# Two of the five sums of convolution weights made by an adding transfer on GpSimd's queue, and a second-level difference moved up on VectorE

## The chip, the cores and the metric

The kernel runs on one core of one Trainium2 chip. Its engines are named as in the profile: PE (TensorE, matrix products), PEld (its weight loads), DVE (VectorE), ACT (ScalarE), POOL (GpSimd) and SP (SyncE, which issues transfers). The metric is the device time of one execution in microseconds; 289.74 us is the median of three runs before the change (289.65 to 289.8).

## The reference, cut to what matters

64 graphs of 128 nodes with 128 features go through a layer norm with ReLU, one graph layer and a residual sum. The part that the change touches is the second convolution of the layer, with 17 taps along the nodes:

```python
h = relu(bn1(conv1d(hT, conv1_w, pad=0)))          # 1 tap
h = bn2(conv1d(h, conv2_w, pad=8))                 # 17 taps, 128 -> 128 channels
x_conv = relu(h + hT)
s = x @ w_se.T + b_se ;  A = exp(-|s_n - s_m|^2) * adj
x_nmp = A @ relu(x @ w_msg.T + b_msg)
# GRU gates r, z, n from [x_conv, x_nmp] and x ; out = x + (1-z)*n + z*h
```

All is fp32. The kernel reaches that accuracy by splitting each factor of a product into a high part (float32r) and a low rest, and makes three products of each (high x high, high x low, low x high).

## The kernel before, in words

The graphs are worked on in 8 groups of 8. Each group's convolution is a two-level fast FIR scheme: instead of 16 taps on every node, sums and differences of weights and of inputs make nine smaller convolutions of four taps (`sub_conv(g, q)`, q from 0 to 8, L1277 to L1306), of which each is 12 or 15 matmuls with 256 columns; tap 16 rides along in some of them. The weights for them stand in `wt_hi` and `wt_lo` and are made once, in the set-up, while group 0 is already under way. They come in 13 lots (`LOTS`, L224 to L238): ACT writes the high part of lot n (`lot_high(n)`, L432 to L448) and DVE the low part (`lot_low(n)`, L786 to L790), which waits for the high part. Of the sources, lots 6, 7, 9 and 10 are raw weights of the tile `w2`; lots 2, 3 and 4 come from `fbb` and `fb`, pairwise sums (three DVE instructions, L1041, L1045, L1047); lots 5 and 8 come from `fab`, the sums of taps 4k+r and 4k+r+2 for r = 0 and r = 1, which DVE makes in two instructions of 128x512 (`sums_of_four(0)` and `sums_of_four(1)`, L1052 to L1063). The tiles `fb`, `fbb`, `fab` and `wg` lie in the tile `gate`, so the profile names them gate.

The input side of the scheme, for group 0: `cp` is the output of the first convolution with padding (ACT, L504); `level2_b` makes `vtb` (two DVE instructions, L842), `level1` makes `u` (L834, L835), `level2_u` makes `vtu` (L848, L849). ACT writes the high parts `v_hi` (`v_high_b`, L508; `v_high_u`, L520), DVE the low parts `v_lo` (`v_low_b`, L851; `v_low_u`, L861). `sub_conv(0, 3)` needs lot 5 and the first `v_low_u`; `sub_conv(0, 4)` the second, which follows ACT's `v_high_u(0, 1)` (L531).

Every engine's order is written out by hand and each engine runs in its order. ACT's around the change: lot 4, two copies `hg` (L474), lot 5, `v_high_u(0, 0)` (L526), `m_shared(0, 0)` (L541), lots 6 to 10, `v_high_u(0, 1)` (L531), messages. DVE's: L1047, lot 1, the first sum of four, lot 2, `v_low_b(0, 0)`, the two of `level2_b`, lot 3, `v_low_b(0, 1)`, lot 4, the second sum of four, `level1`, lot 5, `v_low_u(0, 0)`, `join_b`, lot 6, `level2_u`, `v_low_u(0, 1)`, `join_b`, lot 7, `v_low_u(0, 2)`, lot 8, the eleven small instructions of `distances` (L260 to L279), lot 9, and the joins of the output (L890 to L909). PE between: sub-convolutions 0 to 2, messages (L1236, L1240), 3 to 5, transposes of `slots` (L1251, which need `distances`), 6, distance products (L1264), 7 (which needs the first join L909), 8.

SP issues all big loads at the start, on one queue: two halves of `xin`, `w_a`, taps 0 to 7 of `w2`, taps 8 to 16, `wg` (w_gate), `bias`, `mask`; and once the first rows are normalised `xin` for group 1 and two tiles `xt`. POOL has nothing after the subtraction of `row` at L416 until the variances of group 1 (`ln_scale_first(2)`, L418).

Of the kernel before, what the change touches and what calls it, by code (L numbers as in the profile page):

```python
# [7 lines left out]
ALU = mybir.AluOpType  # L8
# [52 lines left out]
def gnn_kernel(nc, x_first, x_nm, x_t, adj_t, w_in, w_conv, w_gate, par_in, row_in, bias_in, ln_rows, out):  # L61
    ctx = ExitStack()
    with ctx:
        def sb(name, shape, dt=F32):
            return ctx.enter_context(nc.sbuf_tensor(name, shape, dt))

        def sem(name):
            return ctx.enter_context(nc.semaphore(name))
# [63 lines left out]
        w2 = sb("w2", [P, TAPS, P])  # L132
# [5 lines left out]
        fab = early[:, 21 * P:29 * P].rearrange("p (k r c) -> p k r c", r=2, c=P)  # L138
# [7 lines left out]
        xt_landed = [sem(f"xt_landed{i}") for i in range(3)]  # L146
        rows_stored, col_landed = sem("rows_stored"), sem("col_landed")
        out_stored = [sem(f"out_stored{c}") for c in range(NCH)]

        idle_set = sem("idle_set")  # L150
        pool_set, ident_ready, pool_par, par_ready, row_ready, pads_set = (
            sem("pool_set"), sem("ident_ready"), sem("pool_par"), sem("par_ready"), sem("row_ready"),
            sem("pads_set"))
        row_split, sums_ready, wt_hi_ready, wt_lo_ready = (
            sem("row_split"), sem("sums_ready"), sem("wt_hi_ready"), sem("wt_lo_ready"))
# [37 lines left out]
        def every(first, count, step=2):  # L193
            return slice(first, first + step * (count - 1) + 1, step)
# [4 lines left out]
        def cols(c):  # L199
            return slice(c * CW, (c + 1) * CW)  # L200
# [7 lines left out]
        def part_of(pair, p):  # L208
            return pair[0][:, :] if p == 0 else pair[1][:, (p - 1) * QW:p * QW]
# [7 lines left out]
        def stored(k, n=1):  # L217
            return wt_hi[:, k:k + n, :], wt_lo[:, k:k + n, :]

        raw16 = w2[:, 0:16, :].rearrange("p (k r) c -> p r k c", r=4)  # L220
        fbk = fb.rearrange("p (k r) c -> p r k c", r=2)
        fabk = fab.rearrange("p k r c -> p r k c")
# [60 lines left out]
        @block.sync  # L283
        def _(sp):
            sp.dma_start(xin[:, 0:4, :], x_first[0, :, 0:4, :]).then_inc(xh_landed, 16)
            sp.dma_start(xin[:, 4:8, :], x_first[0, :, 4:8, :]).then_inc(x_landed, 16)
            sp.dma_start(w_a[:], w_in).then_inc(wa_landed, 16)
            sp.dma_start(w2[:, 0:8, :], w_conv[:, 0:8, :]).then_inc(w2a_landed, 16)
            sp.dma_start(w2[:, 8:TAPS, :], w_conv[:, 8:TAPS, :]).then_inc(w2b_landed, 16)
            sp.dma_start(wg, w_gate).then_inc(wg_landed, 16)  # L290
            sp.dma_start(bias[:], bias_in).then_inc(bias_landed, 16)
            sp.dma_start(mask[:], adj_t[0]).then_inc(mask_landed, 16)

            def column_rows(g):

                sp.wait_ge(scale_ready, g - 1)

                upto(sp, col_landed, 16 * (g - 2))
                sp.dma_start(ln_rows.rearrange("k (p b) -> p k b", b=GB), scale[:]).then_inc(rows_stored, 16)
                sp.wait_ge(rows_stored, 16 * (g - 1))  # L300

                sp.wait_ge(wt_lo_ready, LOT_OF_GATES)
                if g > 2:
                    sp.wait_ge(hf_ready, NCH * g)
                sp.dma_start(col_ln, ln_rows.unsqueeze(0).broadcast_to([P, 2, GW])).then_inc(col_landed, 16)


            sp.wait_ge(hn_ready, NCH)
            sp.wait_ge(hn_first, 2)
            sp.dma_start(xin[:], x_first[1]).then_inc(x_landed, 16)  # L310
            for g in range(2):
                sp.dma_start(xts[g][:], x_t[g]).then_inc(xt_landed[g], 16)

            sp.wait_ge(a_ready, NCH)
            sp.dma_start(mask[:], adj_t[1]).then_inc(mask_landed, 16)

            sp.wait_ge(hn_ready, 2 * NCH)
            sp.wait_ge(hn_first, 3)
            sp.dma_start(xin[:], x_nm[0]).then_inc(x_landed, 16)

            sp.wait_ge(ht_ps, 2 * NCH)
            sp.dma_start(xts[2][:], x_t[2]).then_inc(xt_landed[2], 16)
            sp.wait_ge(stats_ready, 3)
            sp.dma_start(xin[:], x_nm[1]).then_inc(x_landed, 16)
            column_rows(2)
            for g in range(1, NG):
                sp.wait_ge(out_ready, NCH * (g - 1) + 1)
                sp.dma_start(out[g - 1, :, cols(0)], ob[0]).then_inc(out_stored[0], 16)
                if g + 2 < NG:

                    sp.wait_ge(sum_ready, NCH * g)
                    sp.dma_start(xts[(g + 2) % 3][:], x_t[g + 2]).then_inc(xt_landed[(g + 2) % 3], 16)
                sp.wait_ge(out_ready, NCH * (g - 1) + 2)
                sp.dma_start(out[g - 1, :, cols(1)], ob[1]).then_inc(out_stored[1], 16)
                if g + 1 < NG:
                    sp.wait_ge(a_ready, NCH * (g + 1))
                    sp.dma_start(mask[:], adj_t[g + 1]).then_inc(mask_landed, 16)
                if g + 3 < NG:
                    sp.wait_ge(stats_ready, g + 3)
                    sp.dma_start(xin[:], x_nm[g + 1]).then_inc(x_landed, 16)  # L340
                if g + 2 < NG:
                    column_rows(g + 2)
            for p in range(3):
                sp.wait_ge(out_ready, LAST + p)
                sp.dma_start(out[NG - 1, :, PART_COLS[p]], part_of(ob, p)).then_inc(out_stored[min(p, 1)], 16)
            sp.wait_ge(out_stored[0], 16 * NG)
            sp.wait_ge(out_stored[1], 16 * (NG + 1))

        @block.gpsimd
        def _(pool):  # L350
# [17 lines left out]
            def ln_scale_first(step):  # L368

                tiles = (slice(0, 4), slice(4, GB), slice(0, GB))[step]  # L370
                pool.wait_ge(vpe_first, step + 1)
                if step == 2:

                    pool.wait_ge(hn_ready, NCH)
                    pool.wait_ge(hn_first, 2)
                pool.tensor_tensor(rstd[:, tiles], vpe[:, tiles], neg_half[:, tiles], ALU.pow).then_inc(rstd_first, 1)  # L376
# [37 lines left out]
            pool.wait_ge(row_ready, 4)  # L414
            pool.wait_ge(pool_par, 8)
            pool.tensor_tensor(row[32:33, :], row_raw[32:33, :], row_hi[32:33, :], ALU.subtract).then_inc(row_split, 1)  # L416
            pool.wait_ge(row_split, 3)
            ln_scale_first(2)  # L418
            pool.wait_ge(rstd_first, 3)
# [7 lines left out]
        def _(act):  # L427
# [4 lines left out]
            def lot_high(n):  # L432
                source, first, count = LOTS[n]
                if n == 0:
                    act.wait_ge(wa_landed, 16)
                elif n == 1:
                    act.wait_ge(w2b_landed, 16)
                elif n == 2:
                    act.wait_ge(sums_ready, 3)
                elif n == 5:  # L440
                    act.wait_ge(sums_ready, 4)
                elif n == 6:
                    act.wait_ge(w2a_landed, 16)
                elif n == 8:
                    act.wait_ge(sums_ready, 5)
                elif n == 11:
                    act.wait_ge(wg_landed, 16)
                act.activation(wt_hi[:, first:first + count, :], source, ACT.Copy).then_inc(wt_hi_ready, 1)  # L448
# [194 lines left out]
            ln_rows_first(0)  # L643
            h_rows_first()
            lot_high(1)
            act.wait_ge(pool_par, 5)
            act.wait_ge(pads_set, 2)
# [97 lines left out]
        def _(dve):  # L745
# [92 lines left out]
            def level2_b(g, i):  # L838
                if i == 0:
                    dve.wait_ge(c_ready, NCH * g + NCH)  # L840
                    upto(dve, v_lob_ready, 2 * g)
                dve.tensor_tensor(vtb[:, i], cp[:, every(1 + 4 * i, VN, 4), :], cp[:, every(3, VN, 4), :],  # L842
                                  ALU.subtract).then_inc(vtb_ready, 1)
# [202 lines left out]
            dve.wait_ge(sums_ready, 2)  # L1046
            dve.tensor_tensor(fbb, fb[:, 0:8:2, :], fb[:, 1:8:2, :], ALU.add).then_inc(sums_ready, 1)  # L1047
            lot_low(1)
            raw = w2[:, 0:16, :].rearrange("p (k r) c -> p r k c", r=4)

            def sums_of_four(r):
                dve.tensor_tensor(fabk[:, r], raw[:, r], raw[:, r + 2], ALU.add).then_inc(sums_ready, 1)  # L1052

            sums_of_four(0)
            lot_low(2)
            dve.wait_ge(pads_set, 6)
            v_low_b(0, 0)
            level2_b(0, 0)
            level2_b(0, 1)
            lot_low(3)  # L1060
            v_low_b(0, 1)
            lot_low(4)
            sums_of_four(1)  # L1063
            level1(0)
            lot_low(5)
            v_low_u(0, 0)
# [401 lines left out]
def upto(engine, semaphore, count):  # L1468

    if count > 0:  # L1470
        engine.wait_ge(semaphore, count)
# [42 lines left out]
```

## Time and profile before

| what | value |
|---|---|
| median of three runs | 289.74 us |
| the profiled execution, its own time | 289.65 us |
| its span | 287.5 us |
| granted clock of PE, mean | 0.996 |
| busy share of the span | PE 96%, DVE 87%, ACT 57%, POOL 17% |
| bytes moved | 25.36 MB, of which 4.56 MB in the first 32 us |

The span is the time from the first to the last instruction; 2.15 us of the execution's own time lie outside it. Each engine's busy time is the sum of its instructions; consecutive instructions of one engine overlap by some 0.1 us, so what one instruction costs its engine is the distance between starts, not its duration. "Idle before" is the wait of an engine ahead of an instruction, with the instruction or transfer that ended it.

### The profile page before, as it was taken

To read this page: it belongs to the slowest core of one execution; us is meant where nothing else is said; L and a number is where in the kernel's file an instruction comes from. 1 tells how busy PE (TensorE), PEld (TensorE's weight loads), DVE (VectorE), ACT (ScalarE), POOL (GpSimd) and SP (SyncE) were. 2 spreads that over 40 slices of the span, in tenths; PEclk is the share of its full clock that TensorE was granted. 3 is DMA by queue.
4 is the path that set the end of the run, shared out by engine and by line. 5 is a ranking of instruction groups with operands and counts; after the bars stand their busy time and mean duration, and the time that the engine had idled before them with its cause. 6 is when DMAs were issued, how large, how long until landed. Compare 5 with 4: busy or idle time off the path is not lost.

```text
span 287.5 us, 5282 instructions
## 1 busy us (share of the span) xinstructions
PE 276.3 (96%) x1866; PEld 248.8 (87%) x1866; DVE 249.8 (87%) x565; ACT 164.5 (57%) x271; POOL 49.7 (17%) x110
## 2 busy tenths in 40 slices
PE   7799899999998999999999999999999999999993
PEld 5498886998887998899888998899988998899993
DVE  6998988988998889978998889979898887986565
ACT  3785468745665267555675266563674366561363
POOL 7400020810015002320025002230025000130000
PEclk9999999999999999999999999999999999999998
DMA  7900014534241402532041312523012120001002
GB/s 240 372 22 0 6 70 146 138 135 169 75 148 38 163 23 74 185 105 81 21 195 43 116 69 74 183 72 114 2 67 117 39 74 2 29 7 39 0 2 73
DMA packets 9437, 25.36 MB, mean 88 GB/s; under 512 B 2626, under 2 KB 3140, under 8 KB 8644
## 3 DMA queue, kind: packets, MB, share of 16 engines
q1 hardware_dynamic: 9264, 25.03, 25.0%
q8 instruction: 15, 0.25, 0.3%
q14 instruction: 10, 0.08, 0.1%
q10 hardware_dynamic: 148, 0.01, 0.0%
HBM read 20.79 MB, written 4.24 MB: 87 GB/s over the span
## 4 chain that ended last, share of the span: by engine, by line
PE 67%; DVE 17%; issue 7%; ACT 5%; POOL 2%; DMA 1%; DVEq 0%; ACTq 0%; POOLq 0%
PE ps L1190 20%; PE ps L1192 19%; PE ps L1191 19%; PE ps L1274 4%; PE ps L1240 3%; DVE stats L747 2%; DVE wt_lo L789 2%; ACT wt_hi L448 1%; POOL rstd L376 1%; PE ps L1251 1%; DMA xin<-x_first 1%; DVE aff L945 1%; DVE v_lo L870 1%; DVE y L890 1%; PE ps L1264 1%
## 5 line engine op out<-in xcount | busy, mean ns | idle before, releaser
L1190 PE MATMUL ps<-v_hi,wt_hi 128*128 128x256 f32 x320 | 92.6, 289 | 3.1 <-DVE y L909 1.5
L1192 PE MATMUL ps<-v_hi,wt_lo 128*128 128x256 f32 x320 | 90.1, 282 | 0.0
L1191 PE MATMUL ps<-v_lo,wt_hi 128*128 128x256 f32 x320 | 89.9, 281 | 0.0
L1190 PEld LDWEIGHTS ps<-v_hi,wt_hi 128*128 128x128 f32 x320 | 60.3, 188 | 5.1 <-DVE wt_lo L789 1.8
L1191 PEld LDWEIGHTS ps<-v_lo,wt_hi 128*128 128x128 f32 x320 | 60.3, 188 | 0.3
L1192 PEld LDWEIGHTS ps<-v_hi,wt_lo 128*128 128x128 f32 x320 | 60.2, 188 | 0.0
L382 POOL TENSOR_TENSOR scale<-vpe,neg_half 128x8 f32<-128x8 f32 x6 | 10.6, 1767 | 110.5 <-DVE scale L764 110.5
L1190 PE MATMUL ps<-h_hi,wt_hi 128*128 128x512 f32 (+1 forms) x67 | 26.3, 392 | 0.3 <-DVE h_lo L799 0.2
L1192 PE MATMUL ps<-h_hi,wt_lo 128*128 128x512 f32 (+1 forms) x67 | 25.8, 386 | 0.0
L1191 PE MATMUL ps<-h_lo,wt_hi 128*128 128x512 f32 (+1 forms) x67 | 25.7, 384 | 0.0
L600 ACT ACTIVATE gate<-ps,par 128x512 f32<-128x512 f32 x14 | 9.6, 687 | 20.6 <-PE ps L1192 20.6
L541 ACT ACTIVATE mbs<-ps,par 128x256 f32<-128x256 f32 x24 | 12.0, 501 | 14.9 <-DVE y L890 14.1
L1190 PE MATMUL ps<-n_hi,wt_hi 128*128 128x512 f32 (+1 forms) x51 | 20.0, 393 | 0.0
L1190 PE MATMUL ps<-xc_hi,wt_hi 128*128 128x512 f32 (+1 forms) x51 | 19.6, 384 | 0.0
L1192 PE MATMUL ps<-n_hi,wt_lo 128*128 128x512 f32 (+1 forms) x51 | 19.5, 382 | 0.0
L1191 PE MATMUL ps<-n_lo,wt_hi 128*128 128x512 f32 (+1 forms) x51 | 19.5, 381 | 0.0
L1192 PE MATMUL ps<-xc_hi,wt_lo 128*128 128x512 f32 (+1 forms) x51 | 19.4, 381 | 0.0
L1191 PE MATMUL ps<-xc_lo,wt_hi 128*128 128x512 f32 (+1 forms) x51 | 19.4, 380 | 0.0
L594 ACT ACTIVATE gn<-ps,par 128x512 f32<-128x512 f32 x15 | 10.3, 689 | 13.4 <-PE ps L1192 13.4
L481 ACT ACTIVATE h_hi<-hf 128x512 fp32r<-128x512 f32 x12 | 7.6, 634 | 17.8 <-DVE hf L776 17.8
L909 DVE SCALAR_TENSOR_TENSOR y<-ps,par,y 128x256 f32<-128x256 f32 x32 | 14.8, 480 | 2.8 <-PE ps L1192 1.8
L1274 PE MATMUL ps<-aff,msg 128*128 128x128 f32 x128 | 16.8, 276 | 0.0
(160 smaller groups left out, 613.2 us busy)
## 6 DMA issues: line engine op xcount, KB each, us to landing
w<-ln_rows SPq DMA_DIRECT2D x6, 1024.0 KB, 4.7
mask<-adj_t SPq DMA_DIRECT2D x8, 512.0 KB, 3.4
xt<-x_t SPq DMA_DIRECT2D x8, 512.0 KB, 3.3
out<-gate SPq DMA_DIRECT2D x15, 256.0 KB, 2.0
xin<-x_nm SPq DMA_DIRECT2D x6, 512.0 KB, 3.3
w<-w_conv SPq DMA_DIRECT2D x1, 576.0 KB, 6.4
gate<-w_gate SPq DMA_DIRECT2D x1, 576.0 KB, 7.4
xin<-x_first SPq DMA_DIRECT2D x2, 256.0 KB, 2.9
```

Of the source, the lines that this page charges most:

```text
L382: pool.tensor_tensor(scale[:, 1, :], vpe[:], neg_half[:], ALU.pow).then_inc(scale_ready, 1)
L481: act.activation(h_hi[g % 2][:, cols(c)], hf[g % 2][:, cols(c)], ACT.Copy).then_inc(h_hi_ready, 1)
L541: act.activation(mbs[i][:], ps[:, 0, 0:QW], ACT.Identity, scale=par[:, SC2:SC2 + 1], **bias).then_inc(mbs_ready, 1)
L594: act.activation(gn[c][:], bank(3), ACT.Identity, bias=par[:, HN:HN + 1], scale=0.5).then_inc(ghn_ready, 1)
L600: act.activation(gr[c], bank(4), ACT.Tanh, bias=par[:, HR:HR + 1], scale=0.5).then_inc(r_ready, 1)
L747: return dve.bn_stats(stats[:, j, :], xin[:, j, :])
L909: dve.scalar_tensor_tensor(out=at, in0=quarter(1 + t), scalar=par[:, SC2:SC2 + 1], in1=at, op0=ALU.mult, op1=ALU.add).then_inc(y_ready, 1)
L1190: pe.matmul(dst, wt_hi[:, blk, :], hi, start=start, stop=False)
L1191: pe.matmul(dst, wt_hi[:, blk, :], lo, start=False, stop=False)
L1192: return pe.matmul(dst, wt_lo[:, blk, :], hi, start=False, stop=stop)
L1240: last = pe.matmul(ps[:, first + k, i * MW:(i + 1) * MW], hg[:, 3 * k + i, :], w_a[:, P:P + MW], start=not biased, stop=not biased or i == ...
L1274: last = pe.matmul(ps[:, dst, i * P:(i + 1) * P], msg[:, b, :], aff[:, b, :], start=True, stop=True)
```

## The change

SP gets one more load: taps 4k and 4k+1 go from device memory into `fab`, behind `wg` and ahead of `bias` and `mask`. POOL, behind its subtraction L416, waits until that load has landed and issues a transfer that adds taps 4k+2 and 4k+3 onto `fab` in place. Its completion counts `pair_summed`. ACT waits for it ahead of lot 5; the wait ahead of lot 8 goes. DVE loses both `sums_of_four`, and the first instruction of `level2_b` with the wait for the pads is moved up to where the first of them stood, ahead of lot 2.

```diff
+        pair_landed, pair_summed = sem("pair_landed"), sem("pair_summed")
+        pairs = w_conv[:, 0:16, :].rearrange("p (k r) c -> p k r c", r=4)
...
             sp.dma_start(wg, w_gate).then_inc(wg_landed, 16)
+            sp.dma_start(fab, pairs[:, :, 0:2, :]).then_inc(pair_landed, 16)
             sp.dma_start(bias[:], bias_in).then_inc(bias_landed, 16)
...
             pool.tensor_tensor(row[32:33, :], row_raw[32:33, :], row_hi[32:33, :], ALU.subtract).then_inc(row_split, 1)
+            pool.wait_ge(pair_landed, 16)
+            pool.dma_start(fab, pairs[:, :, 2:4, :], accum_op=ALU.add).then_inc(pair_summed, 16)
             pool.wait_ge(row_split, 3)
...
                 elif n == 5:
-                    act.wait_ge(sums_ready, 4)
+                    act.wait_ge(pair_summed, 16)
                 elif n == 6:
                     act.wait_ge(w2a_landed, 16)
-                elif n == 8:
-                    act.wait_ge(sums_ready, 5)
...
             lot_low(1)
-            sums_of_four(0)
+            dve.wait_ge(pads_set, 6)
+            level2_b(0, 0)
             lot_low(2)
-            dve.wait_ge(pads_set, 6)
             v_low_b(0, 0)
-            level2_b(0, 0)
             level2_b(0, 1)
             lot_low(3)
             v_low_b(0, 1)
             lot_low(4)
-            sums_of_four(1)
             level1(0)
             lot_low(5)
```

In memory both transfers read 1,024 bytes at a stretch (two taps of 128 numbers), four such stretches in each of 128 partitions: 512 KB each.

## Rows read from the trace of the kernel before

**Rows 1.** PE's waits over the whole span: total us, times, longest
```profile
PE ps L1190 <- DVE y L909: 1.5, 2, 0.8
PE ps L1190 <- DVE v_lo L858: 1.4, 1, 1.4
```

**Rows 2.** Chain that ended last, first 32 us: start us, us, what
```profile
18.07 0.64 DVE u L835
...
18.73 0.65 ACT v_hi L526
19.38 0.45 ACT mbs L541
19.83 2.60 ACT wt_hi L448 x5
22.43 0.60 ACT v_hi L531
...
23.06 0.71 DVE v_lo L870
...
30.35 0.10 DVE y L909
```

**Rows 3.** DVE in order of time: start us, us, instruction, [idle before]
```profile
12.30 0.68 DVE L1052 TENSOR_TENSOR gate<-w 128x512 f32<-128x512 f32 x1
13.09 0.69 DVE L789 TENSOR_TENSOR wt_lo<-gate,wt_hi 128x512 fp32r<-128x512 f32 x1
...
14.04 0.77 DVE L842 TENSOR_TENSOR vtb<-cp 128x264 f32<-128x264 f32 x2
...
16.76 0.68 DVE L1052 TENSOR_TENSOR gate<-w 128x512 f32<-128x512 f32 x1
17.36 0.71 DVE L834 TENSOR_TENSOR u<-cp 128x536 f32<-128x536 f32 x1
...
31.75 1.64 DVE L747 BATCH_NORM_STATS2 stats<-xin 128x6 f32<-128x128 f32 x8
```

**Rows 4.** ACT in order of time
```profile
10.99 1.55 ACT L504 ACTIVATE cp<-ps,par 128x512 f32<-128x512 f32 x2 [0.81 <-PE ps L1192]
12.45 0.62 ACT L448 ACTIVATE wt_hi<-gate 128x512 fp32r<-128x512 f32 x1
...
14.23 0.64 ACT L448 ACTIVATE wt_hi<-gate 128x512 fp32r<-128x512 f32 x1
...
16.88 0.63 ACT L448 ACTIVATE wt_hi<-gate 128x512 fp32r<-128x512 f32 x1
```

**Rows 5.** PE in order of time, at its stops
```profile
27.78 0.65 PE L1251 MATMUL ps<-ident,slots 128*128 128x128 f32 x4 [0.47 <-DVE slots L279]
...
30.98 0.36 PE L1190 MATMUL ps<-v_hi,wt_hi 128*128 128x256 f32 x1 [0.77 <-DVE y L909]
```

**Rows 6.** Transfers, first 32 us: KB each, median us from issue to landing
```profile
gate<-w_gate SPq DMA_DIRECT2D x1, 576.0 KB, 7.4
```

**Rows 7.** SP's issues in order of time
```profile
3.05 0.43 SPq L290 DMA_DIRECT2D gate<-w_gate  x1
...
8.97 0.91 SPq L312 DMA_DIRECT2D xt<-x_t  x2
```

**Rows 8.** All 16 transfer engines: stretches 3.2 to 4 (small packets), 10 to 12 us
```profile
DMA packets 162, 0.20 MB, mean 251 GB/s; under 512 B 22, under 2 KB 110, under 8 KB 162
...
DMA packets 208, 0.73 MB, mean 364 GB/s; under 512 B 24, under 2 KB 31, under 8 KB 208
```

**Rows 9.** Transfers, whole span: KB each, median us from issue to landing
```profile
xt<-x_t SPq DMA_DIRECT2D x8, 512.0 KB, 3.3
```

**Rows 10.** POOL in order of time
```profile
8.05 0.98 POOL L399 TENSOR_TENSOR par<-par 128x2 f32<-128x2 f32 x1
8.99 0.19 POOL L400 TENSOR_TENSOR par<-par 128x2 f32<-128x2 f32 x1
...
9.88 1.03 POOL L416 TENSOR_TENSOR row<-row_raw,row_hi 1x396 fp32r<-1x396 f32 x1 [0.17 <-POOL par L403]
```

More of the change, by code:

```diff
@@ L1048, in _ @@
             lot_low(1)
-            raw = w2[:, 0:16, :].rearrange("p (k r) c -> p r k c", r=4)
-            def sums_of_four(r):
-                dve.tensor_tensor(fabk[:, r], raw[:, r], raw[:, r + 2], ALU.add).then_inc(sums_ready, 1)
-            sums_of_four(0)
+            dve.wait_ge(pads_set, 6)
+            level2_b(0, 0)
             lot_low(2)
-            dve.wait_ge(pads_set, 6)
             v_low_b(0, 0)
-            level2_b(0, 0)
             level2_b(0, 1)
```

## The prediction

> **What bounds the kernel now.** I read PE's waits first, then the chain that ended last, then DVE, ACT, PE, the transfers and POOL in order of time for the first 32 us. Over the whole span most of PE's idle time ahead of matmuls lies in the set-up: 1.4 us ahead of the first sub-convolution, 0.5 ahead of the transposes of slots, and 0.8 ahead of sub-convolution 7 (half of the 1.5 shown; the other such wait is of the same kind, later) [rows 1, 5]. After that PE runs nearly without a gap, so a set-up that ends earlier or later moves the end of the kernel by the same amount. The reader is to see in the chain what sets those two later stops: from 18.73 us it lies on ACT without a break (L526, L541, five lots, L531) up to 23.03, and then on DVE up to the join at 30.35 that PE's stop at 30.98 waits for [rows 2, 5]. What starts ACT's stretch is `u`, from DVE's L835. So in the stretch of the change one moment counts: when ACT can start L526, now 18.73.
>
> **Step 1: the first sum goes, a difference comes in its place.** DVE's sum at 12.30 is gone, and the first of the two L842 (0.77 for two, so 0.39) runs there. It needs `cp`, which ACT ends at 10.99 + 1.55 = 12.54, so it takes 12.56 to about 13.0. Lot 2's low part started at 13.09, which is the end of its high part (12.45 + 0.62 = 13.07) and not the end of the sum (12.98) [rows 3, 4]. It starts at 13.09 again, and with it the low part of the first inputs and PE's first sub-convolution. Behind it DVE now has one L842 fewer, 0.38 us; but it then waits for lot 3's high part, 14.23 + 0.64 = 14.87, as it did for 0.06 us before [rows 3, 4]. Value of this step: 0. The cover is ACT's order, and were `cp` later by more than 0.1 us, lot 2 would be late by the same amount; nothing in the change moves `cp`.
>
> **Step 2: the second sum goes.** It stands at 16.76, and `level1` starts at 17.36, so it costs DVE 0.60 us between starts. Lot 4 ahead of it doesn't move. `u` is then ready at 18.71 - 0.60 = 18.11, and ACT, which was done with lot 5 at 17.51 and waited for `u` since, can start L526 at 18.13 if lot 5 is out of the way by then [rows 2 to 4]. ACT's own stretch has no slack, so L531 ends and DVE's v_lo at 23.06 starts 0.60 earlier (`vtu` comes 0.6 earlier too), as do the transposes and the join [rows 2, 5]. The gain of this step alone: 0.60 us, and no more, because the other removed sum was under cover.
>
> **Step 3: lot 5 waits for the adding transfer.** Lot 5 ran at 16.88, with `fab` complete at 12.98. Behind it on ACT stand L526, L541, lots 6 to 10 and L531: the whole chain. Call T the moment the addition is complete. A lot takes ACT 0.52 between starts (2.60 for five) and follows what it waited for by some 0.02 [rows 2], so L526 starts at max(18.13, T + 0.54). Against 18.73: T up to 17.59 gives the full 0.60; T = 18.19 is no change; beyond it each microsecond costs one. PE has cover for lot 5 itself (sub-convolution 3 comes only behind the messages), not for L531.
>
> Now T. The load of w_gate is issued at 3.05 and lands 7.4 later, 10.45 [rows 6, 7]. The new load stands right behind it: 0.524 MB at 364 GB/s is 1.4 us, landing 11.9. Bounds from the stretches: the 251 GB/s of the stretch with small packets gives 2.1 us and 12.55 [rows 8]. I take 11.9, as 1 KB pieces come nearer to 4 KB ones than to a mix with packets under 512 B. POOL is idle since 10.91 [rows 10] and issues at once.
>
> The issue of a transfer by POOL isn't in the trace. SP's cost 0.43 [rows 7]; POOL's first subtraction took 0.98 where the next small sum took 0.19 [rows 10], so that a first use seems to add 0.8. Sum 1.2 us, bounds 0.4 and 2.5 (for a first use that costs some twice as much). I take 1.2.
>
> Fixed latency: a 512 KB load of later groups, with little beside it, lands 3.3 us after issue [rows 9]; less 0.43 for the issue and 1.3 to 1.4 for the bytes leaves 1.5 to 1.6; I take 1.6.
>
> The bytes: as a plain copy 1.4 us of all engines. To add, the transfer must also read 512 KB of `fab`; if that costs as the first read does, 2.8. And it isn't alone: the queue of SP still holds bias, mask, xin and two xt, 2.2 MB, all issued by 9.9 [rows 6, 7] and 5.9 us of work at 364 GB/s from about 11.0 on, so until nearly 17. A transfer with half of the engines' time takes twice its own. So: 1.4 alone as a copy, 2.8 as a copy shared or an addition alone, 5.6 as an addition shared. No row shows which. I take 4.9: the second read and the sharing both have a cause, the sharing may be less than full because some packets overlap. T = 11.9 + 1.2 + 1.6 + 4.9 = 19.6. The ends with the same other terms are 16.1 (a copy alone) and 20.3 (an addition shared).
>
> The Trainium skill, page "DMA: Bandwidth & Descriptors", section "Anatomy of one DMA — SWDGE (gpsimd) path", fits a transfer of this path as 2.0 us plus its bytes over 436 GB/s. By it T would be 11.9 + 3.2 = 15.1 and the whole 0.60 us would be won; that is a fit of copies with nothing beside them, and no row of this trace shows either an addition or this path.
> The same page, section "Rules for kernel authors", says that an accumulating transfer reads its destination first and writes it later. That is the rule that speaks against the change; no run before shows it.
>
> **Sum.** L526 starts at 19.6 + 0.54 = 20.14 instead of 18.73: 1.41 us late. Against the profiled execution's own 289.65 us (span 287.5) that is 291.1; the median of the runs, 289.74, lies 0.1 above it. Bias, mask, xin and xt land 1.4 us and more later than before, near 17 at the latest. The first of them that is read is xin of group 1, at 31.75 [rows 3]; cost 0, and the cover ends only with 14 us of delay. SP's one more issue, 0.43, costs nothing either, the engines being full.
>
> **Rivals.**
> (a) *Shared but cheap, or alone: T at or before 17.6.* An addition at the price of a copy gives 11.9 + 1.2 + 1.6 + 2.8 = 17.5, so -0.6 us, 289.05; the rule of 2.0 us and 436 GB/s ends here as well. For it: step 2's 0.60 is on the chain, and the terms of issue and latency have room below. Against it: the second read of the addition must be as good as free. It decides up to T = 17.6.
> (b) *Near break-even: T from 17.6 to 18.7.* A later queue but a cheap read, or the reverse, 4 us of bytes less a shorter issue: 289.1 to 290.2, say 289.6.
> (c) *The change does more harm: the adding transfer gets the engines only when SP's queue is empty, or the first issue by POOL costs 2.5.* Queue empty near 17.0, then 2.8 of bytes and about 1 to land: T = 20.8, +2.6 us, 292.3.
> (d) *The ring of POOL's queue costs something outside the span* (now 2.15 us lie there); no row bounds it but the 2.15 itself. I give it 0.
>
> **How the numbers follow.** A measurement of this kernel can tell 0.2%, 0.58 us, from no change. Forecast (T 18.7 to 20.5): 0.34; (c): 0.18; (b): 0.20; (a): 0.28. The gain in (a) is 0.60 at most, a hair above the bound, so I put 0.20 of it as faster and 0.08 as no change. Faster 0.20, same 0.28, slower 0.52. Since both signs are possible, the range runs from 289.0 to 292.4; the forecast's own is 290.2 to 291.9.
>
> **What would show it.** DVE: no L1052, L842 once near 12.6, lot 2 at 13.09 as before, L834 at 16.76. ACT: a wait ahead of the fourth 128x512 lot that is ended by a transfer and not by DVE, of about 2.7 us, and the first L526 at T + 0.54. PE: its stops at the transposes and at sub-convolution 4 grow by 1.4. If L526 starts at 18.13, (a) is right; if its idle time is ended by `u`, lot 5 had no part in it. If lot 2 or PE's first sub-convolution moves, step 1 is wrong. A move of the difference between own time and span is (d).

## The result, and the profile after

| | before | after |
|---|---|---|
| median | 289.69 us (6 runs, 289.57 to 289.80) | 291.06 us (6 runs, 290.60 to 291.33) |
| profiled execution, its own time | 289.65 us | 290.78 us |
| its span | 287.5 us | 288.8 us |

The ratio of the runs is 1.0047, with a 95% interval of 1.0035 to 1.0058: slower by 1.0 to 1.7 us, 1.37 us between the medians. The forecast was 291.1.

The chain that ended last, after (start us, us, what; lines of the code are 4 further down than before, PE's 3 further up):

```profile
9.79 1.02 POOL row L420
10.82 1.11 issue
11.94 7.54 DMA gate<-w_conv
19.50 0.63 ACT wt_hi L452
20.13 0.54 ACT v_hi L530
20.67 0.45 ACT mbs L545
21.12 2.60 ACT wt_hi L452 x5
23.74 0.65 ACT v_hi L535
24.41 0.71 DVE v_lo L874
```

From 20.13 on these are the pieces of before [rows 2], of the same length within 0.1 us, and 1.35 us later at the end (24.41 against 23.06). What is new stands ahead of them: 7.54 us of a transfer, from POOL's issue at 11.94 to its landing at 19.48. Before, `u` on DVE stood there.

ACT after, in order of time (the bracket is the idle time ahead and what ended it):

```profile
15.73 1.09 ACT L478 ACTIVATE hg<-ps 128x512 f32<-128x512 f32 x2
19.50 0.63 ACT L452 ACTIVATE wt_hi<-gate 128x512 fp32r<-128x512 f32 x1 [2.69 <-DMA gate<-w_conv]
20.04 0.63 ACT L530 ACTIVATE v_hi<-u 128x528 fp32r<-128x528 f32 x1
```

DVE after, in order of time:

```profile
12.57 0.43 DVE L846 TENSOR_TENSOR vtb<-cp 128x264 f32<-128x264 f32 x1 [0.28 <-ACT cp L508]
13.01 0.69 DVE L793 TENSOR_TENSOR wt_lo<-gate,wt_hi 128x512 fp32r<-128x512 f32 x1
...
14.82 0.69 DVE L793 TENSOR_TENSOR wt_lo<-gate,wt_hi 128x512 fp32r<-128x512 f32 x1 [0.43 <-ACT wt_hi L452]
...
17.28 0.71 DVE L839 TENSOR_TENSOR u<-cp 128x536 f32<-128x536 f32 x1
20.17 0.69 DVE L793 TENSOR_TENSOR wt_lo<-gate,wt_hi 128x512 fp32r<-128x512 f32 x1 [2.18 <-ACT wt_hi L452]
```

Up to 17.3 DVE runs 0.07 to 0.11 us ahead of before, mostly because the first transfer landed 0.07 earlier in this execution (DVE's first wait ended at 3.40 and not at 3.47). With that taken off, lot 2 (13.01 against 13.09) hasn't moved [rows 3]. `u` is ready at 17.99 where it was ready at 18.71 [rows 2]: 0.6 us earlier beyond that lead. ACT could have started its copy of `u` at 18.0; it stood in the wait for `fab` from 16.82 to 19.50 instead, and DVE idled behind it for 2.18 us.

PE after, at its stops:

```profile
14.19 0.36 PE L1187 MATMUL ps<-v_hi,wt_hi 128*128 128x256 f32 x1 [1.39 <-DVE v_lo L862]
25.22 0.36 PE L1187 MATMUL ps<-v_hi,wt_hi 128*128 128x256 f32 x1 [1.46 <-issue]
29.12 0.66 PE L1248 MATMUL ps<-ident,slots 128*128 128x128 f32 x4 [0.46 <-DVE slots L282]
```

The loss is one new stop of 1.46 us ahead of sub-convolution 4. The profile names no releaser for it ("issue"), but sub-convolution 4 waits for the `v_lo` that DVE ended at 24.41 + 0.71 = 25.12, 0.1 us before PE went on. The stop at the transposes is as long as it was [rows 5].

The adding transfer after. First POOL's issue, then all 16 engines in four stretches of 1 us (13 to 14, 14 to 15, 15 to 16 and 16 to 17; a queue's last figure is the share of the 16 engines' time that its packets took):

```profile
11.94 1.51 POOL L422 DMA_DIRECT2D gate<-w_conv  x1 [1.12 <-DMA gate<-w_conv]
```

```profile
q1 hardware_dynamic: 118, 0.43, 104.2%
...
q1 hardware_dynamic: 109, 0.41, 100.8%
q0 software_dynamic: 2, 0.00, 1.4%
...
q0 software_dynamic: 108, 0.11, 69.5%
q1 hardware_dynamic: 55, 0.17, 42.0%
...
q0 software_dynamic: 177, 0.18, 119.0%
```

POOL was done at 13.45. SP's queue (q1) kept all engines until 15, and the addition (q0) had two packets before then. From 15 to 16 the two share the engines while the last of SP's queue goes. Alone from 16 on, the addition moves 0.18 MB in a microsecond, where SP's queue moves 0.43: the engines are busy and move under half as much.

### The profile page after: what moved, and what is told of

It reads as the page before. It is cut to its first block, busy times and chain, and to the rows that moved or that the text cites. A ratio compares the mean times of both kernels' runs of the same rounds, so it can differ in the third digit from the quotient of the medians.

```text
span 288.8 us, 5282 instructions
## 1 busy us (share of the span) xinstructions
PE 275.8 (96%) x1866; PEld 248.5 (86%) x1866; DVE 248.5 (86%) x563; ACT 164.4 (57%) x271; POOL 51.2 (18%) x111
## 4 chain that ended last, share of the span: by engine, by line
PE 66%; DVE 16%; issue 7%; DMA 4%; POOL 3%; ACT 3%; DVEq 0%; POOLq 0%; ACTq 0%
PE ps L1187 19%; PE ps L1189 19%; PE ps L1188 19%; PE ps L1271 4%; PE ps L1237 3%; DMA gate<-w_conv 3%; DVE stats L751 2%; ACT wt_hi L452 1%; DVE wt_lo L793 1%; POOL rstd L380 1%; PE ps L1248 1%; DMA xin<-x_first 1%; DVE aff L949 1%; DVE v_lo L874 1%; DVE y L894 1%
## 5 line engine op out<-in xcount | busy, mean ns | idle before, releaser
L545 ACT ACTIVATE mbs<-ps,par 128x256 f32<-128x256 f32 x24 | 12.0, 501 | 14.9 <-DVE y L894 14.1
L1187 PE MATMUL ps<-xc_hi,wt_hi 128*128 128x512 f32 (+1 forms) x51 | 19.6, 384 | 0.0
L485 ACT ACTIVATE h_hi<-hf 128x512 fp32r<-128x512 f32 x12 | 7.6, 633 | 17.8 <-DVE hf L780 17.8
```

What stands on the lines that cost most here:

```text
L485: act.activation(h_hi[g % 2][:, cols(c)], hf[g % 2][:, cols(c)], ACT.Copy).then_inc(h_hi_ready, 1)
L545: act.activation(mbs[i][:], ps[:, 0, 0:QW], ACT.Identity, scale=par[:, SC2:SC2 + 1], **bias).then_inc(mbs_ready, 1)
L1187: pe.matmul(dst, wt_hi[:, blk, :], hi, start=start, stop=False)
```

## The experiments

My theory after the result: ACT's chain stands behind the landing T of the addition; T is late by two prices, that of adding and that of standing behind SP's queue; and the removed sums were worth 0.6 us, which is lost because T is past 17.6. The rivals: the load or the later landings cost something by themselves; POOL's path is slow whatever the transfer does; DVE's freed time is worth something that no order of the work could have. Each kernel ran beside the kernel before on the same chip, whose medians there were 289.59 to 289.65 us.

**Without the addition** (ACT waits for the load only):

```diff
-            pool.wait_ge(pair_landed, 16)
-            pool.dma_start(fab, pairs[:, :, 2:4, :], accum_op=ALU.add).then_inc(pair_summed, 16)
...
-                    act.wait_ge(pair_summed, 16)
+                    act.wait_ge(pair_landed, 16)
```

> The adding transfer is left out (lots 5 and 8 are then made of taps 4k and 4k+1 alone, not of the sums); ACT waits ahead of lot 5 only for the new load. Theory (the whole loss is the late end of the addition, behind which ACT's chain stands): the load lands near 11.9, lot 5 runs at once behind the two hg copies, L530 starts at 18.05 to 18.13 when u is ready, and the kernel takes 289.1 us, 0.6 less than before. Rival (the new load itself, or the later landings behind it, costs something): 289.7 or more.

Measured: 288.93 us (288.81 to 289.01), ratio 0.9975 [0.9965, 0.9985]. ACT:

```profile
16.79 0.66 ACT L450 ACTIVATE wt_hi<-gate 128x512 fp32r<-128x512 f32 x1
18.13 0.65 ACT L528 ACTIVATE v_hi<-u 128x528 fp32r<-128x528 f32 x1 [0.69 <-DVE u L837]
```

The copy of `u` starts at 18.13. So the load, SP's extra issue and the later landings of mask, xin and xt cost nothing that shows, and DVE's lighter order is worth 0.6 to 0.7 us. The whole loss hangs on T.

**A plain copy on the same path:**

```diff
-            pool.dma_start(fab, pairs[:, :, 2:4, :], accum_op=ALU.add).then_inc(pair_summed, 16)
+            pool.dma_start(fab, pairs[:, :, 2:4, :]).then_inc(pair_summed, 16)
```

> The same transfer on POOL's queue as a plain copy, without the addition (lots 5 and 8 are then made of taps 4k+2 and 4k+3 alone). Theory that adding is what is dear (a 1 KB packet takes about 107 ns of its engine and not about 46): POOL's issue still 1.5 us, the bytes done in 1.5 to 2 us from near 15 on, T = 17.3 to 17.6, 289.1 to 289.2 us. Rival that POOL's path and the queue ahead make T late whatever the transfer does: T above 19, 291.0 us.

Measured: 289.85 us (289.45 to 291.06, 12 runs), ratio 1.0016 [1.0004, 1.0027]. ACT's lot 5:

```profile
18.28 0.63 ACT L452 ACTIVATE wt_hi<-gate 128x512 fp32r<-128x512 f32 x1 [1.41 <-DMA gate<-w_conv]
```

Lot 5 starts at 18.28, so T is 18.26, between the two expectations. POOL's issue took 0.98 us and not 1.51, and the transfer 6.3 us from issue to landing. Four of the twelve runs took 290.57 us or more; the profile is of a quicker one (289.58). The theory had the kind of difference right and its size too large: 1.2 us go to adding and POOL's issue of it, the rest of the lateness stays with a copy.

**The addition with the engines to itself:**

```diff
             sp.dma_start(fab, pairs[:, :, 0:2, :]).then_inc(pair_landed, 16)
+            sp.wait_ge(pair_summed, 16)
             sp.dma_start(bias[:], bias_in).then_inc(bias_landed, 16)
```

> The addition as it is, but SP holds bias, mask, xin and xt back until it has ended, so that it has the transfer engines to itself. Theory that it stands 1.5 us behind SP's queue before its first packet (none before 14.9): packets from about 13.9, 3.4 us of data (16 engines, 32 packets each, 107 ns), T = 17.7 to 18.2, 289.2 to 289.7 us. Rival that its first packets are late by POOL's own path: they start near 15 again, T = 19.2, 290.8 us.

Measured: 289.35 us (289.10 to 290.26, 11 runs), ratio 0.9994 [0.9985, 1.0002]. POOL, and ACT's lot 5:

```profile
11.57 1.51 POOL L423 DMA_DIRECT2D gate<-w_conv  x1 [0.60 <-DMA gate<-w_conv]
```

```profile
18.03 0.63 ACT L453 ACTIVATE wt_hi<-gate 128x512 fp32r<-128x512 f32 x1 [1.07 <-DMA gate<-w_conv]
```

All 16 engines from 13 to 14 us and from 15 to 16:

```profile
DMA packets 22, 0.02 MB, mean 23 GB/s; under 512 B 0, under 2 KB 22, under 8 KB 22
...
q0 software_dynamic: 180, 0.18, 117.1%
```

T is 18.0, inside what was expected. The first packets come at 13.7, 0.6 to 0.7 us behind the issue's end at 13.08, where with the change they came at 14.9, 1.5 us behind it; so 0.8 us of that wait was SP's queue. The transfer takes 6.4 us. It still is an addition: 180 packets of 1 KB in a microsecond of 16 engines. The rival, first packets near 15 whatever stands ahead, is out. A slow start of POOL's path isn't out altogether: the 0.7 us stay, and from 14 to 15 only 105 packets went.

**A copy with the engines to itself** (both edits):

> e3_quiet with a plain copy in place of the addition (lots 5 and 8 are then made of taps 4k+2 and 4k+3 alone): the fourth corner of a square. From issue to landing the transfer took 7.5 us as an addition with the queue beside it, 6.3 as a copy with it, 6.4 as an addition alone. Theory that the price of adding (1.2) and that of the queue (1.1) are separate and add up: 5.1 to 5.3 us here. Rival that one hides the other: 6.2. Both give 289.0 to 289.1 us, T being before 17.6 in either.

Measured: 288.84 us (288.75 to 289.00), ratio 0.9974 [0.9964, 0.9983]. What the transfer took of the 16 engines in the first 32 us, and its issue line (KB, us from issue to landing):

```profile
q0 software_dynamic: 144, 0.52, 5.4%
...
gate<-w_conv POOLq DMA_DIRECT2D x1, 512.0 KB, 4.4
```

4.4 us, and neither 5.1 nor 6.2 as expected. The square, from issue to landing:

| | beside SP's queue | alone |
|---|---|---|
| addition | 7.5 | 6.4 |
| copy | 6.3 | 4.4 |

Adding costs 2.0 us alone and 1.2 beside the queue; the queue costs 1.9 us to a copy and 1.1 to an addition. The prices don't simply add up, and the start shows one reason. The copy beside SP's queue, from 14 to 15:

```profile
q1 hardware_dynamic: 107, 0.41, 99.6%
q0 software_dynamic: 1, 0.00, 1.1%
```

Beside SP's queue the first packet of the addition and that of the copy both came between 14.9 and 15.0, though POOL had ended its issue at 13.45 for the one and at 12.94 for the other: the longer issue of the addition was hidden behind the queue. Alone the copy's first packets came at 13.4, 0.7 us behind its issue. From the first packet to the landing the additions took some 4.6 us beside the queue and 4.3 alone, the copies 3.3 and 2.7. So most of what the queue costs is a later start.

Each of the four numbers is of one profiled execution, and landings scatter. As the loss follows T one for one, the other runs' times give estimates of their T: 19.3 to 20.0 with the change (median 19.8), 18.1 to 19.7 for the copy beside the queue (18.5), 17.8 to 18.9 for the addition alone (18.0). By these medians adding still costs 1.2 us beside the queue, and the queue costs the addition 1.4 rather than 1.1. The copy alone isn't on the chain, so its runs can't be read this way.

The engines' own time fits with the cost of adding: 5.4% of 32 us is 1.7 us of all engines for the copy alone; the addition alone took 11.6% of them, 3.7 us:

```profile
q0 software_dynamic: 528, 0.52, 11.6%
```

Beside SP's queue the copy took 1.5 us of the engines (4.6% of 32). For the addition there, the view of the change's own profile from 12 to 20 us has:

```profile
q0 software_dynamic: 528, 0.52, 42.0%
```

42.0% of 8 us is 3.4 us. The copy also went in fewer pieces, 144 packets where the addition had 528, for the same 0.52 MB. How much of the 3.4 is the adding itself and how much the small pieces was not told apart; the plain load of 1 KB pieces by SP, on another queue, moves as fast as others, which speaks for the adding. All engines with the change, 9 to 11 us, where most packets are of that load:

```profile
DMA packets 614, 0.78 MB, mean 389 GB/s; under 512 B 34, under 2 KB 536, under 8 KB 614
```

**The load ahead of w_gate as well:**

```diff
-            sp.dma_start(wg, w_gate).then_inc(wg_landed, 16)
             sp.dma_start(fab, pairs[:, :, 0:2, :]).then_inc(pair_landed, 16)
+            sp.wait_ge(pair_summed, 16)
+            sp.dma_start(wg, w_gate).then_inc(wg_landed, 16)
```

> As e3_quiet, and the new load goes ahead of w_gate, which is held back too. The load lands near 10.4, POOL is free at 10.8, T comes 1.1 us before that of e3_quiet. Theory (only T counts, up to 17.6): T = 16.6 to 17.1, L530 at 18.05 to 18.13, 289.1 us and not less. Rival (w_gate, landing near 20, or the other late loads become the wait): a new wait of ACT ahead of its lot 11 or of DVE at the stats, 290 us or more.

Measured: 288.98 us (288.80 to 289.40, 7 runs), ratio 0.9978 [0.9967, 0.9988]. POOL issues at once, ACT has `fab` before it wants it and waits for `u` as in the first experiment (POOL's issue, and the transfer's us to landing; then ACT):

```profile
10.94 1.04 POOL L423 DMA_DIRECT2D gate<-w_conv  x1
...
gate<-w_conv POOLq DMA_DIRECT2D x1, 512.0 KB, 5.7
```

```profile
16.85 0.65 ACT L453 ACTIVATE wt_hi<-gate 128x512 fp32r<-128x512 f32 x1
18.19 0.64 ACT L531 ACTIVATE v_hi<-u 128x528 fp32r<-128x528 f32 x1 [0.69 <-DVE u L840]
```

This is the change made to work: T at 16.6 (5.7 us after the issue), and the gain is within 0.05 us that of leaving the addition out. That T decided is so shown from both sides.

**The kernel before, with one sum moved.** Then the question of whether a transfer was needed. First only the second sum, behind `level1`:

```diff
-            sums_of_four(1)
             level1(0)
+            sums_of_four(1)
             lot_low(5)
```

> The kernel before, with one edit: the second sum of four stands behind level1 and not ahead of it. Theory that u alone isn't enough: ACT's L526 starts 0.6 us earlier (18.13), but DVE has the same work up to level2_u, so vtu still ends near 22.3 and L531 and DVE's first v_lo behind it keep their times: 289.65 us, no change. Rival that u starts the chain whatever else DVE does: 289.05 us.

Measured: 289.44 us (289.31 to 289.68), ratio 0.9995 [0.9986, 1.0003]. No change that can be told. But the mechanism shows, with a part that I hadn't expected:

```profile
18.07 0.64 ACT L526 ACTIVATE v_hi<-u 128x528 fp32r<-128x528 f32 x1 [0.62 <-DVE u L835]
...
22.12 1.18 ACT L531 ACTIVATE v_hi<-vtu 128x528 fp32r<-128x528 f32 x2 [0.35 <-DVE vtu L849]
```

ACT starts its copy of `u` 0.6 earlier and then waits 0.35 for `vtu` at its other end. L531 starts at 22.12 against 22.38 before (0.06 of it is this execution's earlier start); the 0.2 us won are a wait of DVE for ACT ahead of its low part of `u` (19.41, where the step before it ended 0.2 sooner), which an earlier ACT takes away. I had overlooked it. A second edit takes what held the rest:

```diff
             join_b(0, 0)
-            lot_low(6)
             level2_u(0)
+            lot_low(6)
```

> As e5_move, and the low part of lot 6 stands behind level2_u (where DVE sat idle for 0.71 us) and not ahead of it. Theory: vtu ends 0.6 us earlier too, L531 starts at 21.8 and DVE's v_lo at 22.45: 289.0 us, the whole gain of the change without a transfer. Rival that DVE's work, 0.6 us more than with the transfer, binds: 289.5 us or more.

Measured: 288.92 us (288.80 to 289.02), ratio 0.9975 [0.9966, 0.9985]. ACT's copy of `vtu` now waits for nothing:

```profile
21.61 1.17 ACT L531 ACTIVATE v_hi<-vtu 128x528 fp32r<-128x528 f32 x2
```

As expected: the gain of the early addition (0.67 us by the medians), with both sums on DVE and no transfer. The freed 0.6 us of DVE weren't what the removal of the sum was worth; its place ahead of `u` was. No run moved lot 6 alone. In the kernel before, ACT's L531 followed its lots without a wait for `vtu`, so that move by itself should win nothing there; this isn't shown.

**Lot 6 into ACT's idle time**, on both (with `lot_low(6)` behind `level2_u`):

```diff
             lot_high(5)
+            lot_high(6)
             v_high_u(0, 0)
             m_shared(0, 0)
-            for n in range(6, 11):
+            for n in range(7, 11):
```

On the version without a transfer:

> e6_move2 with lot 6 ahead of the copy of u on ACT: no new transfer at all, both sums on DVE. Theory: DVE has no idle time left, its chain starts 0.75 to 0.9 us earlier than before: 288.8 us, and the transfer of e8_early_lots is worth 0.3 us over it. Rival that DVE's 0.6 us of the sum comes back in full: 289.1 us.

Measured: 288.82 us (288.75 to 288.88), ratio 0.9973 [0.9962, 0.9984]. And on the early addition:

> e4_early with two reorderings: ACT makes lot 6 in its idle time ahead of L531 (the copy of u), and DVE's low part of lot 6 stands behind level2_u. Theory that ACT's chain is what DVE waits for (0.71 us idle): the copy of vtu starts near 21.3, the DVE chain is some 0.5 us earlier than in e4_early, 288.5 us. Rival that PE binds by then (its stop at the transposes had already gone in e4_early): 288.9 us, as e4_early.

Measured: 288.28 us (288.24 to 289.49, 6 runs, four of them at 288.24 to 288.31), ratio 0.9965 [0.9952, 0.9977]: the fastest of all, 1.3 us below the kernel before by the medians, 1.0 by the ratio, which the two later runs pull up. DVE's low part of `vtu`, first without, then with the transfer:

```profile
22.18 0.71 DVE L871 TENSOR_TENSOR v_lo<-vtu,v_hi 128x528 fp32r<-128x528 f32 x1
```

```profile
21.79 0.71 DVE L876 TENSOR_TENSOR v_lo<-vtu,v_hi 128x528 fp32r<-128x528 f32 x1
```

Here, and only here, the freed time of DVE counts: v_lo is 0.39 us earlier with the transfer, and the medians differ by 0.54. Without the transfer the wait that ACT's reordering removed comes back as one for `vtu` (0.27 us ahead of L531), and only 0.1 us is won over the version above; I had expected 0.15 to 0.3 there, and 0.3 and not 0.54 between the two. PE's stop ahead of sub-convolution 7 shrinks to 0.47 with the transfer and stays 0.75 without.

## Why the prediction was right, step by step

- *Step 1 (the first sum is under cover), forecast 0.* Right: lot 2's start is set by ACT, and DVE's gain comes back as idle time, 0.28 us ahead of L846 and 0.43 ahead of lot 3, where before it was 0.06.
- *Step 2 (the second sum is worth 0.60).* Right. The experiments without an addition and with an early one gained 0.72 and 0.67 us by the medians, and the chain started 0.60 and 0.54 earlier (18.13 and 18.19 against 18.73). That `vtu` had to come along was said only in a bracket; the one-sum experiment showed it to be a condition of its own.
- *Step 3, T = 19.6, measured 19.48.* Right in the sum, less so in its terms, which missed by 0.3 and 0.5 us in opposite directions. POOL's issue started at 11.94 (forecast 11.9; the load had landed at 11.6). It took 1.51 us (forecast 1.2, from SP's 0.43 and a first use of 0.8). A copy's took 0.98 after the same kind of wait, but the early addition's 1.04 without one. So adding by itself doesn't set it, and whether a first use does was not tested. The rest, latency and bytes, took 6.0 us where 1.6 + 4.9 were set.
- *How the two queues meet, in step 3.* This step came out at the right number in part by luck. I had the addition share the engines with SP's queue until nearly 17. The queue in fact had them to itself until the addition's first packets at 14.9, shared them for less than a microsecond, and was empty soon after 15.5 (four packets from 16 to 17). This is nearer to rival (c), in which the addition gets the engines only when SP's queue is empty. (c) set T at 20.8 because it had the queue empty at 17.0, from 2.2 MB at 364 GB/s; the queue moved 0.39 to 0.43 MB a microsecond and had 1.8 MB left at 11. The addition then took 3.4 us of all engines, above the 2.8 of a second read as fast as the first. A queue that is 1.5 us shorter and an addition that is 0.6 us dearer than in (c) give a T near that of the forecast.
- *The loss follows T one for one.* Right: L530 at 20.04, 0.54 after T + 0.02, and PE 1.34 late at the transposes (29.12 against 27.78). But I named the stops at the transposes and at sub-convolution 4 as those that grow; only the second did (0 to 1.46), since PE and DVE were late together afterwards.
- *Rival (a)*, an addition at a copy's price, decides up to T = 17.6: the copy beside the queue missed that (T 18.26, and 18.1 at the least by its runs' times), so it wouldn't have held even with free adding. The rule of the Trainium skill, page "DMA: Bandwidth & Descriptors", section "Anatomy of one DMA — SWDGE (gpsimd) path", 2.0 us plus bytes over 436 GB/s, gives 3.2 us; the measured 4.4 for a copy alone and 7.5 for the addition beside the queue are above it. That an accumulating transfer reads its destination (the Trainium skill, the same page, section "Rules for kernel authors") fits with the engines' time of 3.4 and 3.7 us against 1.5 and 1.7, but no run shows the read by itself.
- *Rival (d)*, time outside the span: 290.78 - 288.8 = 2.0 against 2.15. Nothing.

## What to carry to other kernels

A transfer that takes work off an engine must land before the first instruction that stands behind it in any engine's order, not before its data is needed: here lot 5 had over 4 us of cover on PE (its high part was ready at 17.51 before, and PE read it at 21.85) and 0.7 on ACT (T up to 17.59, against a start at 16.88). Ask first whether the removed instruction is worth something for its time or for its place; if for its place, moving it costs nothing, and here it brought the same 0.7 us without a transfer. And a transfer on a second queue isn't alone: in this kernel it stood behind the rest of SP's queue (1.8 MB at 11 us), which could have waited, and holding them back brought its landing 1.5 us forward, 1.1 of it by the transfer itself and 0.4 by the earlier landing of its load.

## What the runs showed of the hardware that was not expected

- An addition of 512 KB in 1 KB pieces took 3.4 us of all 16 engines beside SP's queue and 3.7 alone; a copy of the same bytes on the same path took 1.5 and 1.7 us, in 144 packets and not 528.
- A transfer issued by POOL beside a full queue of SP got its first packet at 14.9 to 15.0, 1.5 us (addition) and 2.0 us (copy) behind the end of its issue, while SP's queue held 99 to 104% of the engines. With SP's queue held back it was 0.6 to 0.7 us.
- POOL's issue took 1.51 us for the addition and 0.98 for the copy; for the two early additions, issued straight behind POOL's own work, it took 1.04 and 1.09. Why is open.
- A kernel whose chain hangs on the landing of such a transfer scatters: 290.60 to 291.33 with the change, 289.45 to 291.06 with the copy, 289.10 to 290.26 alone on the engines, against 289.50 to 289.89 before. Without the addition, with the copy alone on the engines and with both sums on DVE (the two orders that gained) it was 288.75 to 289.02. The early addition has two runs of seven at 289.25 and 289.40, and the fastest version two of six at 289.03 and 289.49, so both may at times be reached by a late landing; their profiles were of executions at 289.02 and 288.31, and this is left open.
